# An embedding bag on one core: eighteen features by counting and fourteen by gathering, instead of twenty and twelve

## The reference

```
flat   = tables.reshape(F*V, E)
emb    = flat[ids + arange(F)[None, :, None] * V]          # (512, 32, 20, 64)
mask   = arange(20) < lengths[..., None]
pooled = einsum('bfle,bfl->bfe', emb, mask)
out    = nan_to_num(pooled.reshape(512, 32 * 64))
```

## Time and profile before

| | |
|---|---|
| median of three runs | 1046.8 us |
| profiled execution | 1047.35 us |
| its span, first to last instruction | 1045.4 us |
| outside the span | 1.95 us |
| mean granted clock of TensorE | 0.997 of full speed |
| indirect gathers L432, puts L442, scatters L407 | 495, 48, 48 |

### The profile page before, as it was taken

How to read it: one execution, slowest core, us unless ns; L and a number is a source line. 1 busy time by engine, 2 the same in 40 slices (tenths; PEclk the granted TensorE clock), 3 DMA queues, 4 the chain that set the end, 5 groups by cost and what they waited for, 6 DMA issues and landing times.

```text
span 1045.4 us, 29010 instructions
## 1 busy us (share of the span) xinstructions
PE 983.3 (94%) x9885; PEld 864.1 (83%) x9885; DVE 937.4 (90%) x2485; ACT 754.1 (72%) x1121; POOL 666.0 (64%) x617
## 2 busy tenths in 40 slices
PE   3499999999999999999999999999999999999996
PEld 0188888888888888888888888888888888888885
DVE  9987879898999989999989998999999898999980
ACT  2477777878686868787777777787868686877770
POOL 3874677676676756777667767767676775773010
PEclk9999999999999999999999999999999999999998
DMA  6234142534444343535252626244443434241300
GB/s 220 82 136 118 37 141 67 152 111 131 128 120 135 115 141 105 161 86 179 69 171 76 188 59 191 75 148 119 129 133 115 146 106 116 76 115 50 106 28 6
DMA packets 66140, 119.85 MB, mean 115 GB/s; under 512 B 31600, under 2 KB 33351, under 8 KB 66065
## 3 DMA queue, kind: packets, MB, share of 16 engines
q1 hardware_dynamic: 45696, 100.66, 30.0%
q0 software_dynamic: 19168, 17.93, 8.5%
q10 hardware_dynamic: 1200, 0.58, 0.2%
HBM read 83.45 MB, written 4.71 MB: 84 GB/s over the span
## 4 chain that ended last, share of the span: by engine, by line
PE 79%; DVE 16%; ACT 2%; issue 1%; DVEq 1%; POOL 0%; POOLq 0%
PE sums L530 55%; PE pairs L520 18%; PE rest L548 6%; DVE onehot_j L746 5%; DVE gathered L804 3%; DVE onehot_p L744 2%; ACT table L487 1%; DVE table L755 1%; DVE table L763 1%; ACT counts L475 1%; DVEq L800 1%; DVE is_nan L772 0%; DVE gathered L775 0%; DVE counts L636 0%; DVE j_of L688 0%
## 5 line engine op out<-in xcount | busy, mean ns | idle before, releaser
L530 PE MATMUL sums<-table,counts 128*128 128x192 bf16 x7840 | 806.7, 247 | 0.0
L475 ACT ACTIVATE counts<-pairs 128x588 int16<-128x588 f32 (+1 forms) x880 | 563.7, 651 | 239.5 <-PE pairs L520 232.8
L530 PEld LDWEIGHTS sums<-table,counts 128*128 128x128 fp8e3 x7840 | 690.1, 96 | 44.4 <-issue 0.2
L432 POOL DMA_INDIRECT rows<-tables,row_now x495 | 553.3, 1118 | 245.6 <-PE pairs L520 128.9
L746 DVE TENSOR_SCALAR onehot_j<-ramp,j_of,worth 128x296 bf16<-128x296 f16 x1680 | 491.9, 355 | 0.0
L520 PE MATMUL pairs<-onehot_j,onehot_p 128*128 128x294 bf16 x1720 | 364.6, 292 | 40.6 <-DVE onehot_j L746 28.3
L520 PEld LDWEIGHTS pairs<-onehot_j,onehot_p 128*128 128x128 bf16 x1720 | 159.5, 97 | 101.0 <-issue 27.9
L744 DVE TENSOR_TENSOR onehot_p<-ramp,p_of 128x768 bf16<-128x768 f16 x280 | 153.7, 549 | 72.7 <-PE pairs L520 71.9
L804 DVE TENSOR_REDUCE gathered<-rows 128x64 f32<-128x1280 f32 x48 | 114.3, 2381 | 3.5 <-issue 3.5
L442 POOL DMA_INDIRECT out_gathered<-gathered,place_now x48 | 52.4, 1091 | 69.3 <-issue 67.1
L548 PE MATMUL rest<-table,minus_eye 128*128 128x448 bf16 x320 | 91.5, 367 | 3.6 <-ACT rest L483 1.6
(11 more groups left out here) (67 smaller groups left out, 83.3 us busy)
## 6 DMA issues: line engine op xcount, KB each, us to landing
table<-tables SPq DMA_DIRECT2D x140, 448.0 KB
rows<-zeros SPq DMA_DIRECT2D x48, 640.0 KB
rows<-tables,row_now POOLq DMA_INDIRECT x495
out_counted<-pooled SPq DMA_DIRECT2D x120, 21.0 KB
rows<-lookup_ids SPq DMA_DIRECT2D x1, 817.0 KB, 8.2
rows<-lookup_lengths SPq DMA_DIRECT2D x1, 817.0 KB, 9.7
sorted_records<-records,rank POOLq DMA_INDIRECT x48
out_gathered<-gathered,place_now POOLq DMA_INDIRECT x48
```

The lines of the kernel that those rows point to most:

```text
L432: nc.gpsimd.indirect_dma_start(out=rows[:, k, l * E:(l + 1) * E], out_offset=None, in_=table_rows, in_offset=bass.IndirectOffsetOnAxis(ap= ...
L475: nc.scalar.activation(dst, src, ACT.Copy).then_inc(counts_saved, 1)
L530: last = nc.tensor.matmul(sums[h][:, k * PARTS * E:(k + 1) * PARTS * E], counts[h][:, j, :, k], parts[:, :, j, :, 1], start=(j == 0 and k ...
```

## The change

Two features move from counting to gathering. M is 18, so there are 18 x 14 = 252 stages and 18 x 44 = 792 evictions, and 4 x 14 = 56 tiles in seven rounds of the eight buffers. The pace is 96 evictions for a round instead of 125, 24 for a pair instead of 31, one for each id position instead of 7/5, and it starts at eviction 45 instead of 72. Tile t is added at stage 41 + 15t // 4 instead of 41 + 5t, the last one (t = 55) at stage 247. GpSimd's loop covers bodies 1 to 5, and body 6 and the puts of body 6 stand behind it. The scratch arrays for the ranking are made for 56 tiles.

```diff
-M = 20
+M = 18
-FIRST_ADD = 41
-ADD_EVERY = 5
-FIRST_GATHER = 72
-PAIR_OF_TILES = 31
-PER_BODY = 125
+FIRST_GATHER = 45
+PAIR_OF_TILES = 24
+PER_BODY = 96
+
+def add_stage(t):
+    return 41 + 15 * t // 4
 def since(l):
-    return 7 * l // 5
+    return l
...
-    added_at = {divmod(FIRST_ADD + ADD_EVERY * t, STAGES): t for t in range(TILES)}
+    added_at = {divmod(add_stage(t), STAGES): t for t in range(TILES)}
...
             body(0, True)
-            with pool.Fori(1, BODIES) as b:
+            with pool.Fori(1, BODIES - 1) as b:
                 body(b, False)
+            body(BODIES - 1, False, LAST_BODY)
+            for x in range(LAST_BODY // SLOTS, 2):
+                put(BODIES - 2, x)
+            for x in range(LAST_BODY // SLOTS):
+                put(BODIES - 1, x)
             for x in range(2):
-                put(BODIES - 1, x)
...
-                nc.vector.tensor_scalar(later[:], depth_f, -1.4, PAIR_OF_TILES - 2.0, ALU.mult, ALU.add)
+                nc.vector.tensor_scalar(later[:], depth_f, -1.0, PAIR_OF_TILES - 2.0, ALU.mult, ALU.add)
```

More of the change, by code:

```diff
@@ L110, in build_embedding_bag @@
     LAST_WORDS = LAST_BAGS // 2
-    BODIES = TILES // BUFFERS
+    BODIES = -(-TILES // BUFFERS)
+    COLUMNS = BODIES * BUFFERS
+    LAST_BODY = TILES - (BODIES - 1) * BUFFERS
     STAGES = 2 * CHUNKS
-    assert TILES % BUFFERS == 0 and BUFFERS % 2 == 0 and BODIES > 1
+    assert LAST_BODY in (SLOTS, BUFFERS) and BUFFERS % 2 == 0 and BODIES > 1
     assert J % CHUNKS == 0 and GROUPS * GROUP >= HALF and PER_CHUNK % 2 == 0 and CHUNKS * PER_CHUNK == LAST
@@ L123, in build_embedding_bag @@
     STORES = 2 * TRIO + LAST_WORDS
-    added_at = {divmod(FIRST_ADD + ADD_EVERY * t, STAGES): t for t in range(TILES)}
-    assert FIRST_ADD + ADD_EVERY * (TILES - 1) < M * STAGES
+    added_at = {divmod(add_stage(t), STAGES): t for t in range(TILES)}
+    assert add_stage(TILES - 1) < M * STAGES
     LEFT = TILES
@@ L165, in build_embedding_bag @@
         rank = sb("rank", [P, TILES], I32)
-        depth = sb("depth", [P, TILES], I32)
-        later = sb("later", [P, TILES], I32)
-        arrival = sb("arrival", [P, 2, TILES], I32)
+        depth = sb("depth", [P, COLUMNS], I32)
+        later = sb("later", [P, COLUMNS], I32)
+        arrival = sb("arrival", [P, 2, COLUMNS], I32)
         is_nan = sb("is_nan", [P, max(BLOCKS, SLOTS) * E], U8)
@@ L196, in build_embedding_bag @@
         value = piece(L + 1)
-        last_rank = piece(TILES)
+        last_rank = piece(COLUMNS)
         length = piece(TILES, F32)
-        has = piece((L + 1) * TILES, F32)
+        has_room = piece(max((L + 1) * TILES, L * COLUMNS), F32)
+        has = has_room[:, 0:(L + 1) * TILES]
         until = piece((L + 1) * TILES, F32)
@@ L203, in build_embedding_bag @@
         below = piece(L + 1, F32)
-        rank_f, depth_f = piece(TILES, F32), piece(TILES, F32)
-        runs_f = until[:, 4 * TILES:(4 + L // 4) * TILES].rearrange("p (t q) -> p t q", t=TILES)
-        turn_f, arrival_f = (until[:, 2 * x * TILES:2 * (x + 1) * TILES].rearrange("p (x t) -> p x t", x=2) for x in range(2))
+        rank_f, depth_f = piece(TILES, F32), piece(COLUMNS, F32)
+        runs_f = until[:, 4 * COLUMNS:(4 + L // 4) * COLUMNS].rearrange("p (t q) -> p t q", t=COLUMNS)
+        turn_f, arrival_f = (until[:, 2 * x * COLUMNS:2 * (x + 1) * COLUMNS].rearrange("p (x t) -> p x t", x=2)
+                             for x in range(2))
         halves = piece(P + L + 1).bitcast(F16)
@@ L444, in put, with body @@
                         in_=gathered[:, k * E:(k + 1) * E], in_offset=None).then_inc(gathered_stored[x], 16)
-            def body(b, first):
-                for k in range(BUFFERS):
+            def body(b, first, tiles=BUFFERS):
+                for k in range(tiles):
                     if not first and k % SLOTS == PUT_AT:
@@ L452, in _ @@
             body(0, True)
-            with pool.Fori(1, BODIES) as b:
+            with pool.Fori(1, BODIES - 1) as b:
                 body(b, False)
+            body(BODIES - 1, False, LAST_BODY)
[3 more added lines that the diff above has]
+                put(BODIES - 1, x)
             for x in range(2):
-                put(BODIES - 1, x)
-                pool.wait_ge(gathered_stored[x], 16 * SLOTS * BODIES)
+                pool.wait_ge(gathered_stored[x], 16 * SLOTS * (BODIES - 1 + (x < LAST_BODY // SLOTS)))
         @block.scalar
@@ L655, in find_depths @@
             def find_depths():
-                fits = has[:, 0:TILES * L].rearrange("p (t l) -> p t l", l=L)
-                step(nc.vector.tensor_tensor(fits, below[:, 1:L + 1].unsqueeze(1).to_broadcast([P, TILES, L]),
-                                             last_rank.unsqueeze(2).to_broadcast([P, TILES, L]), ALU.is_le))
+                fits = has_room[:, 0:COLUMNS * L].rearrange("p (t l) -> p t l", l=L)
+                step(nc.vector.tensor_tensor(fits, below[:, 1:L + 1].unsqueeze(1).to_broadcast([P, COLUMNS, L]),
+                                             last_rank.unsqueeze(2).to_broadcast([P, COLUMNS, L]), ALU.is_le))
                 step(nc.vector.tensor_reduce(out=depth_f, in_=fits, axis=AX_X, op=ALU.add))
```

## The result

The changed kernel takes 1058.24 us (median of 4 runs, 1057.14 to 1058.94), the kernel before 1046.82 us beside it: 1.0107 times as long, 95% interval 1.0094 to 1.0119. It is 1.1% slower. The time lies in the stated range (1030 to 1062), 10 us over the forecast of 1048 and 0.2 past the end of the forecast's own 1038 to 1058.

The account below looks back on a forecast made before the run. GpSimd, 90% full, was taken to set the time: start at 110 plus 871.9 us of list put tile 54's landing at 984.4; 62.3 to the end and 1.95 outside the span made 1048.6, 1048 against the median; range 1030 to 1062.

Parts of the forecast that it names:

- The bound: GpSimd, 90% full, not 64%, issues without a break until its last gather; the 99 us TensorE saves turn into waits.
- the extra: Gather time over the median, beside VectorE's cuts: 3.66 us a feature when GpSimd is never idle, 57.5 us up to tile 54.
- rival B: Extra goes with the gathers (65 us instead of 57.5), or is 1.2 times when GpSimd never rests: 1056 to 1060; chance 0.12.
- The tail: From the add of tile 54 to the end: 62.3 us, the same sequence as in the kernel before.
- The add of tile 54: Stage 243: comes when its rows have landed, at 984.4, 97 us later than without GpSimd.
- Buffers and puts ... no wait: GpSimd's eight buffers: add of tile 0 at 172, GpSimd reaches tile 8 at about 228; later seven buffers always ahead: 0.
- The sign that the prediction named: Among the signs of a right forecast: VectorE's adds wait for rows, from about tile 17 on.
- Rival A: TensorE's clock falls in the stalls; two low-level stages a pair cost 32 us, 1080, one at the end alone 1052; chance 0.12.
- C: Most of the gathers' extra goes as waiting VectorE leaves GpSimd alone: down to 991, half of it 1020; chance 0.08.
- D: GpSimd keeps the pace of 27.0 us a pair: 948, with VectorE's 16 us 964; chance 0.04.
- the two big amounts: TensorE's saving of 99 us and the add of tile 54 coming 97 us later; they nearly cancel by chance.

Follow-up runs that it names:

- the run with the puts at 0: The changed kernel with the four puts ahead of the first and fifth tile of a body instead of the third and seventh: 1049.68 us, ratio 1.0033.

## Why the prediction was right, and where not

**The bound: right.** That GpSimd is 90% full and would take the chain, so that two features of TensorE's work buy nothing, is what the runs show. The first gather was expected at 110 and came at 111.2. The last gather of tile 54 was expected to end at 981.6 (871.9 us of work from 110, less a gap) and ended at 982.6. That the sum met within a us is partly luck. Up to tile 54 the extra was 63.7 us over the median of the 571 gathers, 6 more than the term of 57.5 and near the 65 of rival B; against it the 48 puts took 47.3 us instead of 48 x 1.091 = 52.4, and the gathers' median was 1.002 instead of 1.004, another 1.1. That the extra goes with the cuts was right for two thirds of it. Rival B (all of it each gather's own) is excluded by the run without cuts, though the measured time lies in the 1056 to 1060 that it gave: those us came from the puts.

**The tail: right.** From the add of tile 54 to the end 62.3 us were taken from the kernel before; it was 61.9.

**The add of tile 54: wrong by 11 us.** It was expected at 984.4, with its rows, and came at 995.3. The step that failed is "Buffers and puts ... no wait". It asked whether GpSimd waits for a buffer (it doesn't), took it that "an add follows its tile at once", and did not ask whether VectorE waits for the puts: the `gathered_stored` wait is in the code of `add_rows`, it is never seen in the trace of before, because there the puts were through long before the adds, and so I gave it no price. In the kernel before, the last put that the add of tile 44 needs, in GpSimd's timeline, and that add, in VectorE's, lie 32 us apart:

```profile
918.39 0.96 POOL L442 DMA_INDIRECT out_gathered<-gathered,place_now  x1 [0.30 <-PE pairs L520]
...
950.62 2.41 DVE L804 TENSOR_REDUCE gathered<-rows 128x64 f32<-128x1280 f32 x1
```

With GpSimd late by its whole list, it makes the add of each fourth tile wait for that tile's gathers, the next tile's and four puts. From tile 52 on, held until 971.97, VectorE and TensorE had 7 stages and the adds of tiles 52 and 53 to do until the add of tile 54; that took 23.4 us and was no longer covered. With the puts out of the way this add came at 985.16, and the run at 1049.7, 1.7 us over the forecast. The sign that the prediction named, adds that wait for rows from about tile 17 on, was half right: from tile 16 on adds waited, but every fourth one, and for the puts.

**Rival A: the fall was there, the price was not.** The granted clock of the whole run was 0.956, and it fell where A said, in the idle times behind long waits of VectorE. The windows of after, in the standstill ahead of the late add of tile 52, behind TensorE's restart, and then:

```profile
964.40:968.60 4.20, 0.00 (x0) 0.00 (x0) 0.00 (x0) 0.00 (x0) 3.05 (x4) 0.99 0.07 20
968.60:975.10 6.50, 0.00 (x0) 0.00 (x0) 3.13 (x5) 0.00 (x0) 4.98 (x6) 0.50 0.12 25
975.10:978.80 3.70, 3.69 (x22) 3.04 (x23) 3.70 (x14) 1.33 (x2) 2.92 (x3) 0.51 0.16 27
...
982.00:995.30 13.30, 13.30 (x141) 12.12 (x139) 10.99 (x30) 9.62 (x15) 10.25 (x11) 1.00 0.51 132
```

TensorE stood still for about 11 us, up to 975.1. The granted clock was 0.50 over the last 6.5 of them, the 1.2 GHz level, still 0.51 over the first 3.7 us of work, and 1.00 from 982.0 on. The rule of the Trainium skill in TensorE: Matmul & The Clock Gate, section HAM oscillation, says that such bursts start throttled; the trace agrees. What this stretch cost is bounded by VectorE's waits for TensorE between the adds of tiles 52 and 54, 0.30 + 0.99 + 1.28 = 2.6 us, and not all of that is the clock. In the run with the puts at 0 the clock was 0.964, and from the add of tile 54 to the end were 62.9 us instead of 62.3. While GpSimd sets the time, a slow stretch of TensorE is paid from time in which it would have waited.

**Rivals C and D: out.** The mean gather, 1.112 us, hardly moved from 1.118, though VectorE rested more; no gather ran at the pace of the list.

**The verdict.** The forecast lay 1.2 us over the median before and the result 11.4. Slower had the largest of the three chances, 0.42, but 0.22 of that came from rivals A and B, and neither came about as it was priced. That the two big amounts nearly cancel held (the forecast is within 1.7 us of the kernel with the puts out of the way). The sign doesn't rest on the missed wait: that kernel too is slower than the one before, by 3.4 us (ratio 1.0033, interval 1.0021 to 1.0044). The wait made the 3.4 us 11.4. The forecast, 1.2 us over the median, could not have told the sign.

## What to carry to other kernels

When work is moved from a full engine to one that looks two thirds busy, count the second engine's instructions with the gaps between them and take its own pacing waits out: here 64% was 90%, and one feature fitted where two did not. What lengthens the second engine's instructions counts too: here the instructions that VectorE ran beside a gather. Then list every wait in both directions between the two engines, the ones that the trace never shows above all: a wait that has always been met early (here for a buffer to be stored) has no row, and becomes the chain as soon as the engine behind it falls late. Where such a wait is met by an instruction in an ordered list, move that instruction ahead of the work it need not stand behind. Here that was worth about 8 us (11.4 us over the kernel before became 3.4).

## What the runs showed of the hardware that was not expected

One chip ran all four kernels that were run on it slower, and not in proportion. The kernel before took 1279 us on it (1.22 times), nineteen features 1320 (1.32 times), the kernel without cuts 1366 (1.35 times), the changed kernel with the loosened pace 1722 (1.62 times its 1060 on another chip). From the waits of that last run on that chip:

```profile
ACT counts L484 <- remote: 591.4, 71, 21.2
DVE onehot_p L753 <- remote: 501.2, 37, 32.0
```

These are idle times ended by nothing that the core's own trace shows. The gathers were no slower (mean 1.018 us, 1.114 in the same kernel on the other chip). The mean granted clock was 0.782, but the median matmul of L539 took 247 ns, as in the changed kernel. Whether the pace, which holds nothing back in the run above, matters there isn't known: between the two 18-feature runs on that chip, 1366 and 1722 us, both the cuts and the pace differ, so this isn't separated, and what is slow on that chip stays open.
